# Twenty engine loops of a one-core Trainium2 kernel written out as straight code

## The reference

```python
x = L0_attn_x
x = _layernorm(x + _L0_attn_ref(x, ...), axis=-1)   # l0a: Mamba-2 chunked scan, 4 heads of 128
x = _layernorm(x + _L0_ffn_ref(x, ...), axis=-1)    # l0f: int8 gate/up/down, 256 -> 1024 -> 256
x = _layernorm(x + _L1_attn_ref(x, ...), axis=-1)   # l1a: attention, 16 heads of 128
x = _layernorm(x + _L1_ffn_ref(x, ...), axis=-1)    # l1f: 32 experts, top 4
x = _layernorm(x + _L2_attn_ref(x, ...), axis=-1)   # l2a: Mamba selective scan
x = _layernorm(x + _L2_ffn_ref(x, ...), axis=-1)    # l2f: ternary gate/up/down, rms norm
x = _layernorm(x + _L3_attn_ref(x, ...), axis=-1)   # l3a: attention with one shared key/value head, and an MLP
x = _layernorm(x + _L3_ffn_ref(x, ...), axis=-1)    # l3f: gated MLP of 688 with low-rank experts, top 2
```

```python
# L3_attn: HIDDEN 256, 16 heads of 16, one shared key/value
h = _ln(x, ln1_g, ln1_b)
q = (h @ wq + bq).reshape(B, S, N_HEADS, HEAD_DIM)
kv = h @ wkv + bkv
k, v = (kv[..., :KV_DIM], kv[..., KV_DIM:])
scores = jnp.einsum('bshd,btd->bhst', q, k) * scale
scores = jnp.where(causal, scores, jnp.finfo(scores.dtype).min)
probs = jax.nn.softmax(scores, axis=-1)
attn = jnp.einsum('bhst,btd->bshd', probs, v).reshape(B, S, H)
...
# L3_ffn: 8 experts of rank 8, top 2
gate = x @ W_gate + _lora(x, sA_gate, sB_gate, scale) + _expert_lora(x, A_gate, B_gate, w, scale)
up = x @ W_up + _lora(x, sA_up, sB_up, scale) + _expert_lora(x, A_up, B_up, w, scale)
hidden = jax.nn.silu(gate) * up
out = hidden @ W_down + _lora(hidden, sA_down, sB_down, scale) + _expert_lora(hidden, A_down, B_down, w, scale)
```

## Time and profile before

| | us |
|---|---|
| median of the three runs | 2662.49 |
| profiled execution, own time | 2687.0 |
| its span in the trace | 2685.3 |
| PE busy | 2271.4 (85%) |
| DVE busy | 1702.8 (63%) |
| ACT busy | 1443.0 (54%) |
| POOL busy | 781.0 (29%) |
| mean granted TensorE clock | 0.917 of full speed |

### The profile page before, as it was taken

The page is one execution under the profiler, slowest core; times in us unless marked ns, Lnnn a source line. Parts: engine busy times, 40 slices in busy tenths (PEclk is TensorE's granted clock), DMA queues, the critical chain, the costliest instruction groups (busy, mean ns, idle before and its releaser), DMA issues. The chain is left out here.

```text
span 2685.3 us, 48369 instructions
## 1 busy us (share of the span) xinstructions
PE 2271.4 (85%) x15926; PEld 1964.0 (73%) x15926; DVE 1702.8 (63%) x4081; ACT 1443.0 (54%) x3765; POOL 781.0 (29%) x796
## 2 busy tenths in 40 slices
PE   6996869999999817999458888999686898987997
PEld 5875868999999716999346666777586576766886
DVE  4675777888888525553358888878365666563443
ACT  4664547887878402333266767776232666663332
POOL 1111010000000260000438888768485222211000
PEclk9888999999999758999779989999797999998999
DMA  4000110000000472333311111010300000000000
GB/s 128 1 0 15 48 48 32 1 2 3 2 3 2 136 223 91 118 113 99 111 56 44 47 42 48 33 51 15 112 1 0 1 1 1 0 0 0 1 0 31
DMA packets 77912, 111.42 MB, mean 41 GB/s; under 512 B 15482, under 2 KB 64242, under 8 KB 76676
## 3 DMA queue, kind: packets, MB, share of 16 engines
q1 hardware_dynamic: 70212, 87.23, 10.1%
q0 software_dynamic: 7488, 21.50, 2.6%
HBM read 79.73 MB, written 28.97 MB: 40 GB/s over the span
## 5 line engine op out<-in xcount | busy, mean ns | idle before, releaser
L1858 POOL TENSOR_TENSOR l2a_hb<-l2a_hb,l2a_Cb 128x1024 f32<-128x1024 f32 x128 | 303.3, 2379 | 111.7 <-DVE l2a_hb L2314 110.8
L2314 DVE TENSOR_TENSOR_SCAN l2a_hb<-l2a_dA,l2a_dB 128x1024 f32<-128x1024 f32 x128 | 288.4, 2275 | 62.5 <-PE l2a_dB L1939 28.8
L2168 ACT ACTIVATE l2a_dA<-l2a_delta,l2a_An 128x255 f32<-128x255 f32 x512 | 214.3, 497 | 37.5 <-DVE l2a_delta L2254 20.9
L1939 PE MATMUL l2a_dB<-l2a_diag,l2a_dxT 64*128 64x128 f32 x2048 | 191.9, 309 | 31.9 <-DVE l2a_hb L2314 19.1
L1939 PEld LDWEIGHTS l2a_dB<-l2a_diag,l2a_dxT 64*128 64x128 f32 x2048 | 141.8, 197 | 96.3 <-PE l2a_dB L1939 37.8
L901 PE MATMUL l1a_QK<-l1a_xh,early_wqkv_h 128*128 128x256 f32 x512 | 144.2, 282 | 5.1 <-issue 3.6
L1959 PE MATMUL l2a_YS<-ident,l2a_hb 128*128 128x128 f32 x1024 | 143.8, 287 | 1.0 <-POOL l2a_hb L1858 1.0
L901 PE MATMUL l1a_QK<-l1a_xl,early_wqkv_h 128*128 128x256 f32 x512 | 143.2, 280 | 0.0
L901 PE MATMUL l1a_QK<-l1a_xh,early_wqkv 128*128 128x256 f32 x512 | 143.1, 280 | 0.0
L1099 ACT ACTIVATE l1a_ex<-l1a_S,l1a_nm 128x256 f32<-128x256 f32 x256 | 119.1, 471 | 38.1 <-DVE l1a_nm L1151 38.1
L1959 PEld LDWEIGHTS l2a_YS<-ident,l2a_hb 128*128 128x128 f32 x1024 | 117.8, 147 | 12.5 <-issue 1.5
(11 more groups left out here) (616 smaller groups left out, 7483.7 us busy)
## 6 DMA issues: line engine op xcount, KB each, us to landing
l2a_Cb<-c_rows SPq DMA_DIRECT2D x8, 2048.0 KB
l1f_xl<-moe_x_rows SPq DMA_DIRECT2D x95, 128.0 KB, 2.0
moe_y_rows<-l1f_yo SPq DMA_DIRECT2D x95, 128.0 KB, 1.7
l0f_raw<-in_L_attn_w_qkv_dram SPq DMA_DIRECT2D x24, 256.0 KB, 2.9
moe_x_rows<-X SPq DMA_DIRECT2D x1, 4224.0 KB, 17.3
l1f_dL<-in_L_ffn_Wd_dram SPq DMA_DIRECT2D x1, 3072.0 KB
X<-in_L_attn_x_dram SPq DMA_DIRECT2D x8, 256.0 KB, 6.0
l1a_raw<-in_L_attn_w_o_dram SPq DMA_DIRECT2D x4, 512.0 KB, 4.5
```

Source lines behind the costliest of these rows:

```text
L1858: nc.gpsimd.tensor_tensor(h[:, :, :], h[:, :, :], Cb[p][:, s0:s0 + UN, :], ALU.mult).then_inc(hc_ready, 1)
L1939: last = nc.tensor.matmul(out[:, m:m + 2, j * P + a:j * P + a + HP], dxT[q][a:a + HP, j, c * P:(c + 1) * P], diag[q][a:a + HP, j, s0 + m:s ...
L2168: last = nc.scalar.activation(dA[(i * NU + u) % DAS][:, n, 1:SEQ], delta[q][:, c, 1:SEQ], ACT.Exp, scale=An[:, c, s0 + n:s0 + n + 1])
L2314: nc.vector.tensor_tensor_scan(flat(hb[u % RING]), flat(dA[(i * NU + u) % DAS]), dB[u % 2][:, :], 0.0, ALU.mult, ALU.add).then_inc(scanned, 1)
```

## The change

In l0a, l0f, l2f, l3a and l3f the loops of POOL, PE, ACT and DVE, twenty in all, become Python loops: the program holds the instructions of every item. l1a's loop stays. The twenty edits are all of this form (two of them shown):

```diff
@@ -428,7 +428,7 @@
             item(1, 1)
-            with pe.Fori(1, ITEMS // 2 - 1) as it:
+            for it in range(1, ITEMS // 2 - 1):
                 for p in range(2):
                     item(it * 2 + p, p)
...
@@ -3236,7 +3236,7 @@
             item(1, 1)
-            with pe.Fori(1, ITEMS // 2) as it:
+            for it in range(1, ITEMS // 2):
                 for p in range(2):
                     item(it * 2 + p, p)
```

More of the change, by code:

```diff
@@ L296, in _ @@
             item(1, 1)
-            with pool.Fori(1, ITEMS // 2 - 1) as it:
+            for it in range(1, ITEMS // 2 - 1):
                 for p in range(2):
@@ L538, in _ @@
             item(1, 1, early=True)
-            with act.Fori(1, ITEMS // 2 - 1) as it:
+            for it in range(1, ITEMS // 2 - 1):
                 for p in range(2):
@@ L702, in _ @@
             item(1, 1)
-            with dve.Fori(1, ITEMS // 2 - 1) as it:
+            for it in range(1, ITEMS // 2 - 1):
                 for p in range(2):
@@ L770, in _ @@
             item(1, 1)
-            with pool.Fori(1, ITEMS // 2) as it:
+            for it in range(1, ITEMS // 2):
                 for p in range(2):
@@ L841, in _ @@
             item(1, 1)
-            with act.Fori(1, ITEMS // 2) as it:
+            for it in range(1, ITEMS // 2):
                 for p in range(2):
@@ L887, in _ @@
             item(1, 1)
-            with dve.Fori(1, ITEMS // 2) as it:
+            for it in range(1, ITEMS // 2):
                 for p in range(2):
```

## The result

The changed kernel takes 2655.20 us (median of 14 runs, 2651.67 to 2662.69), the kernel before 2665.06 in 14 runs on the same chip (2659.95 to 2673.02). The ratio is 0.9964, 95% interval 0.9952 to 0.9976: 9.9 us faster, with 6.4 to 12.8 in the interval. A second comparison, of 11 runs, gave 0.9958 (0.9942 to 0.9973). The forecast was a saving of 6.4 us.

The account below looks back on a forecast made before the run. PE was taken to set the time, its idle spots over register instructions or branches being what counts. Terms -2.5 - 1.4 - 1.7 - 0.8 = -6.4 us took 2662.5 to 2656.1 us; range 2647 to 2664.

Parts of the forecast that it names:

- rival D: Granted clock in l2f, l0a, l3f: shifted idle times could remove dips, 6.0 us more, 2650.1 us in all; chance 0.13.
- Step 1: l1a on PE: its loop moves in the instruction list, so the second stall behind each branch back goes, -2.5 us.
- The guard for DVE's border: l1a on DVE: its moved loop start may give DVE a second stall; one of 1.3 us has cover.
- Step 2: l3f on PE: register operations between a wait and the transposes XT go, -1.4 us over six items (1.1 to 1.7).
- Step 3: l3a on DVE: register and address operations between softmax steps go, 0.28 us an item, -1.7 us (0 to 5.0).
- Step 4: l0a, l0f, l2f: register operations once an item in l0f and l0a, nothing in l2f; -0.8 us (0 to 2).
- B: Waits hidden anyway: l1a keeps both stalls, l3a's gain is lost; only -1.4 to -2.2 us left, 2660.7 us; chance 0.20.
- C: Changed stages: fetching straight code stalls PE at block borders, +16 us, 2678 us; chance 0.11 together with a DVE stall.
- E: Strict fetch rule: each of nine removed branches back cost 3.3 us, so 30 us more gain, 2626 us; chance 0.02.

Follow-up runs that it names:

- the two paddings: Kernel before, all loops kept, with 40 or 16 idle PE instructions ahead of l1a: ratio 0.9999 with 40, 2680.51 us (one execution) with 16.
- the single-engine runs: Changed kernel with the five loops kept on one engine only: DVE ratio 0.9972, PE ratio 0.9968, POOL 2668.07 us (one execution).

## Why the prediction held, and where it didn't

*Sign and size.* Forecast 6.4 us, measured 9.9 (6.4 to 12.8). The range held 2655.2. That the level was met so closely (2656.1 forecast) is partly luck: the three first runs had a median 2.6 us below that of all fourteen (2662.49 against 2665.06), which made up for most of the 3.5 us by which the saving was too small. The terms are these, in us:

| term | forecast | measured (items of the profiles) |
|---|---|---|
| l1a, second stall | 2.5 | 2.5: stalls of 1.26 and 1.20 gone; the items gained 1.45 and 2.1, with chance in the first stall (1.5 to 2.2) |
| l3f, XT | 1.4 | 1.1: six items of 24.10 to 23.91 |
| l3a, DVE | 1.7 | 1.4 |
| l0a, l0f | 0.8 | 0.7 to 1.0: l0f with what follows 0.6 and 0.7, l0a 0.1 and 0.3 |
| l2f, POOL | 0 | 1.2: six items of 15.26 (mean with POOL's loop alone) to 15.05 |
| l2f, clock dips | 0 (rival D) | 0.6 to 1.2: one or two times 0.6 (15.9 to 15.3) |
| l3f, clock dips at its start | 0 (rival D) | 1.5 to 4.5 in the two profiles of before, 0 in those of after |

The four terms that were forecast came to 5.7 to 6.0 of their 6.4 us. What the profiles add to that, 3.3 to 6.9 us, stands in the three rows that were put at 0.

*Step 1* was right in mechanism and in size, and the two paddings show it in both directions. One number in it was wrong (80 for 54, since the built program isn't what PE fetches); both put the border far behind the start, which was luck. For the same reason the bodies that branch back without a stall reach up to 1129 instructions and not 737, and the list of PE grows in the trace by 5646 different instructions, 22 blocks, and not 17.8. The guard for DVE's border was not needed: with DVE's loops kept (its loop at the old place) and without, PE has one stall.

*Step 2.* Right; 0.19 per item was the lower bound, since 0.55 was a single outlier among five of 0.45 to 0.46.

*Step 3.* Right in engine, and 1.4 for 1.7 in size. Of the 0.23 us an item, 0.14 are PE's wait for `sm` (0.57 to 0.43) and 0.09 its wait for `ex` (0.73 to 0.64); which of DVE's places gave them, the two in front of the statistics and `residual` as forecast or the ones behind `nm`, no run separates. I had said that this wait would have to fall below 0.3 for step 3 to be too small; it fell only to 0.43.

*Step 4* failed in l2f. It read 15.21 us from 1966.16 to 1981.37 as a straight item and found the loop equally long. But line 2532 handles item i inside the code of item i+1, so both ends of that stretch lay in the loop already, and of the 15.15 us before it the later end did; the kernel before holds no straight item by this marker. And I had not asked which engine sets l2f. POOL is busy 12.87 of 15.90 us there, and PE's 13.55 are that many only because its clock is low; POOL's register operations stand between squares and sums, and 0.08 us at some five places became 0.21 us an item.

*The rivals.* B is refuted by each of the single-engine runs. C: no stall that could be a fetch shows in the straight items. PE does have waits marked "issue" there, 1.55 us once an item in l2f, but the kernel before waits 1.77 at the same matmul, and 0.25 once an item in l0a in one of the two profiles of the changed kernel; in the changed kernel 20 more packets came on q8 and the straight items are shorter; with l1a straight PE's list grows by 8724 instructions over the kernel before, and no item of l1a pays for it. D, "I see no reason for either sign", had a sign: l2f's dips came with its loops (15.8 and 16.4 in the run that kept them, none in the six full items of the nine profiles with straight code on all engines or a loop on only some). E is refuted: in l3a and l3f an item with a branch is no longer than one without. In l0f and l2f a branch back does cost something, which the prediction put at nothing: the stretches in which POOL branches back are 0.07 to 0.08 us longer (15.31 against 15.23 in l0f of the kernel before, 15.29 against 15.22 in l2f with POOL's loop), a fortieth of the 3.3 us that E needs. Of a border crossed in sequence the Trainium skill ("Runtime: NRT & Kernel Launch", section "Instruction fetch mechanics") says that it is mostly hidden; the straight items of l1a agree, 59.96 to 60.00 us each, with some four borders in every one.

*Open.* Why l3f has a slow item near its start in all four profiles of kernels with every loop (the first item with 28.43, 25.42 and 25.46; in the fourth the second and third, 27.34 and 28.61) and in one of the ten others (the second item with 28.71). It is a granted clock of 0.57 from 2516 to 2526 in the kernel before, after two PE waits of 1.04 and 0.27 us that are the same in the changed kernel. Neither l3f's loops nor PE's nor DVE's bring it back reliably. With four against ten profiles it may be the shifted timing of the stages ahead; no run shows that. It is worth some 3 us by the two profiles of before (4.5 and 1.5), a third of the measured gain, and so the largest uncertain part of it. The terms are read from two profiles of each kernel; that the timed runs split the same way is not shown.

## What to carry to other kernels

A loop whose body stays in the engine (up to 1129 instructions on PE here) costs its register operations and next to nothing for its branches (at most 0.08 us). The register operations count only where the next operation would follow directly, or waits for the one that comes last, on the engine that sets the pace (0.08 us for one between two operations of DVE or POOL, 0.19 ahead of PE's transposes; find that engine stage by stage). A loop body that no longer fits (2145 here) pays 1.5 to 2.2 us per branch back, and 0.9 to 2.1 more if a block border comes soon behind its start (it did at 31 and 15 instructions, not at 57), so an edit anywhere ahead of it can gain or lose some 2.5 us in code that it doesn't touch. When straight and loop items are compared in a trace, take the stretch by the code in which its two ends lie, not by the item they belong to.

## What was not expected of the hardware

- An instruction with two waits whose semaphore has long reached its value took PE 0.109 us: the idle time grew from 9.90 to 24.73 us when 136 more were put in.
- With PE stalls of 1.84 and 2.10 us and five matmuls between them the granted clock fell to 0.50 (1.2 of 2.4 GHz) as the second began, and was back at 1.00 after 658. With 1.52 and 1.26 us and 13 matmuls between them it stayed at 1.00. One single stall of 1.89 us was followed by 0.50 as well (767.6 to 770.9), others of up to 2.23 us by 1.00.
- The stall directly behind a branch back in l1a is 1.49 to 2.23 us long in the profiles here, varying by chance. Written out, the same border takes nothing.
- The instruction lists of PE, DVE, ACT and POOL grew by 6086 instructions together as built, the fetched volume grew from 2.69 to 3.12 MB over the span, and the time fell.
